# Adjacency pass of a four-layer graph network: the raw row blocks of a pair loaded by one 3 MB transfer instead of two of 1.5 MB

## The reference

```python
h = jnp.maximum(_layernorm(x, axis=-1), 0.0)
# layer 0, with e made from h by small 64 x 64 products
h = adj @ (adj.T @ e)                    # then a layer norm, gamma, beta, + residual
# layer 1
x = x + adj @ h
# layer 2: Chebyshev sum, three products by adj
T_curr = adj @ x; T_next = 2.0 * (adj @ T_curr) - T_prev    # k = 2, 3
# layer 3
a = adj + eye(n); degree = jnp.sum(a, axis=1); d_is = degree ** -0.5
out = jnp.maximum((d_is[:, None] * a * d_is[None, :]) @ (h @ W + b), 0.0)
```

## Time and profile before

| | |
|---|---|
| median of 3 runs | 1551.16 us (1549.36 to 1553.0) |
| profiled execution, its own time | 1554.13 us |
| its span, first to last instruction | 1552.3 us |
| PE busy | 1485.6 us, 96% of the span |
| DVE, ACT, POOL busy | 379.7, 256.7, 84.4 us |
| chain that ended last | PE 81%, DMA 14%, of it `raw<-in_adj_dram` 9% |
| bytes moved | 532.66 MB, 343 GB/s over the span |
| mean granted PE clock | 0.987 of full speed |

### The profile page before, as it was taken

How to read it: one execution, slowest core, us unless ns; L and a number is a source line. 1 busy time by engine, 2 the same in 40 slices (tenths; PEclk the granted TensorE clock), 3 DMA queues, 4 the chain that set the end, 5 groups by cost and what they waited for, 6 DMA issues and landing times.

```text
span 1552.3 us, 17963 instructions
## 1 busy us (share of the span) xinstructions
PE 1485.6 (96%) x7901; PEld 632.2 (41%) x7901; DVE 379.7 (24%) x383; ACT 256.7 (17%) x510; POOL 84.4 (5%) x67
## 2 busy tenths in 40 slices
PE   6998989989898989999999999999999999999996
PEld 3554545545454655323333333333333333333331
DVE  5683443434344332311101100000100021100210
ACT  2233324333333435000000000000000000000000
POOL 2300000000000004600000000000000000000000
PEclk9999999999999999999999999999999999999999
DMA  9897998979798989999999977779798845788997
GB/s 329 318 398 295 414 361 335 381 311 403 296 397 315 361 331 394 421 421 420 420 421 400 328 317 291 291 296 388 264 349 293 289 156 235 295 333 348 385 419 307
DMA packets 103218, 532.66 MB, mean 343 GB/s; under 512 B 19389, under 2 KB 19429, under 8 KB 55269
## 3 DMA queue, kind: packets, MB, share of 16 engines
q1 hardware_dynamic: 96052, 529.84, 87.1%
q10 hardware_dynamic: 7088, 1.67, 0.5%
HBM read 425.32 MB, written 106.17 MB: 342 GB/s over the span
## 4 chain that ended last, share of the span: by engine, by line
PE 81%; DMA 14%; ACT 1%; POOL 1%; DVE 1%; issue 0%; SPq 0%; ACTq 0%; POOLq 0%; DVEq 0%
PE turned L465 30%; PE acc L465 29%; PE t_acc L476 10%; PE turned L491 9%; DMA raw<-in_adj_dram 9%; DMA over_last<-adj_t 5%; ACT staged L676 1%; PE t_acc L606 1%; POOL rstd L981 1%; DMA w_in<-in_L_gnn_W_i_dram 0%; PE turned L632 0%; PE turned L638 0%; PE t_rows L616 0%; PE acc L517 0%; POOL E L998 0%
## 5 line engine op out<-in xcount | busy, mean ns | idle before, releaser
L676 ACT ACTIVATE staged<-turned 128x512 f32<-128x512 f32 x400 | 204.2, 615 | 275.0 <-PE turned L491 270.7
L809 DVE TENSOR_REDUCE deg_part<-raw 128x4 f32<-128x3072 f32 (+1 forms) x70 | 222.7, 3197 | 82.8 <-DMA raw<-in_adj_dram 82.8
L476 PE MATMUL t_acc<-raw,E 128*64 128x384 f32 (+1 forms) x1120 | 200.3, 504 | 28.1 <-DMA raw<-in_adj_dram 27.9
L491 PEld LDWEIGHTS turned<-ident,raw 128*128 128x128 f32 x1600 | 173.8, 140 | 42.6 <-issue 40.2
L491 PE MATMUL turned<-ident,raw 128*128 128x128 f32 x1600 | 190.7, 275 | 0.0
L465 PE MATMUL acc<-staged,t_cur 128*64 128x512 f32 x800 | 186.9, 601 | 2.7 <-ACT t_cur L713 1.5
L465 PE MATMUL turned<-over_last,C 128*64 128x512 f32 x680 | 153.4, 593 | 0.0
L476 PEld LDWEIGHTS t_acc<-raw,E 128*64 128x64 f32 x1120 | 82.6, 145 | 143.8 <-issue 90.5
L465 PE MATMUL turned<-over_last,R 128*64 128x512 f32 x568 | 130.4, 595 | 4.1 <-DMA over_last<-adj_t 4.1
L465 PE MATMUL acc<-over_last,R 128*64 128x512 f32 x504 | 115.3, 595 | 4.6 <-DMA over_last<-adj_t 3.3
L981 POOL TENSOR_TENSOR rstd<-rstd,minus_half 128x8 f32<-128x8 f32 (+1 forms) x30 | 43.8, 1461 | 1349.7 <-DVE rstd L800 1349.7
(11 more groups left out here) (125 smaller groups left out, 760.4 us busy)
## 6 DMA issues: line engine op xcount, KB each, us to landing
over_last<-adj_t SPq DMA_DIRECT2D x203, 1024.0 KB, 12.3
raw<-in_adj_dram SPq DMA_DIRECT2D x60, 1536.0 KB, 13.7
adj_t<-staged SPq DMA_DIRECT2D x60, 1536.0 KB, 12.7
staged<-adj_t SPq DMA_DIRECT2D x80, 1024.0 KB, 10.7
over_wide<-adj_t SPq DMA_DIRECT2D x21, 1024.0 KB, 10.3
raw<-in_adj_dram SPq DMA_DIRECT2D x10, 1024.0 KB, 10.3
adj_t<-staged SPq DMA_DIRECT2D x10, 1024.0 KB, 10.3
out_dram<-sq ACTq DMA_DIRECT2D x5, 256.0 KB, 30.4
```

The costliest lines, as they stand in the source:

```text
L476: last = nc.tensor.matmul(t_acc[h * D:(h + 1) * D, 0:columns], E[:, m * SUB + a, :], raw_of(g, m)[:, a, h * columns:(h + 1) * columns], st ...
L491: last = nc.tensor.transpose(turned[q % TURN_BANKS][:, a * P:(a + 1) * P], raw_of(g, u // 2 * 2 + b)[:, sub, c * P:(c + 1) * P], ident[:, :])
L676: nc.scalar.activation(staged_of(g, u)[:, i * B:(i + 1) * B], turned[q % TURN_BANKS][:, :], ACT.Copy) \
L809: nc.vector.tensor_reduce(deg_part[:, of(m), g], raw_of(g, m), AX.X, ALU.add).then_inc(deg_summed, 1)
```

## The change

`load_next(g, m)` now loads both blocks m and m+1 by one transfer. It is issued where the load of the even block stood, before the odd unit's store; the second load behind the store is gone. The transfer waits for the degree sum of the odd block (which comes last of the two), and both blocks' readers, PE (L476) and DVE (L809), wait for the one semaphore of the even block. The first group is loaded as before.

```diff
+        def raw_landed(g, m):
+
+            return raw_in[m if g == 0 else m // 2 * 2], 16 * (g + 1)
...
             def load_next(g, m):
 
-                sp.wait_ge(chunk_turned, chunk_no(g, m // 2 * 2 + 1, chunks(g)))
-                sp.wait_ge(deg_summed, SUM_NO[g, m])
-                src = adj_v[:, m, :, (g + 1) * GW:(g + 1) * GW + chunks(g + 1) * P]
-                sp.dma_start(raw_of(g + 1, m), src).then_inc(raw_in[m], 16)
+                sp.wait_ge(chunk_turned, chunk_no(g, m + 1, chunks(g)))
+                sp.wait_ge(deg_summed, SUM_NO[g, m + 1])
+                dst = raw_last if g + 1 == NG - 1 else raw
+                src = adj_v[:, m:m + 2, :, (g + 1) * GW:(g + 1) * GW + chunks(g + 1) * P]
+                sp.dma_start(dst[:, m:m + 2], src).then_inc(raw_in[m], 16)
...
                         load_next(g, u - 1)
                         store(g, u)
-                        load_next(g, u)
...
             def products_for_t(g, m):
 
-                pe.wait_ge(raw_in[m], g * 16 + 16)
+                pe.wait_ge(*raw_landed(g, m))
...
             def sum_rows(g, m):
 
-                dve.wait_ge(raw_in[m], g * 16 + 16)
+                dve.wait_ge(*raw_landed(g, m))
```

## The result

| | us | against before |
|---|---|---|
| before, median | 1550.74 (1549.36 to 1553.0) | |
| changed kernel, median of 4 | 1587.21 (1578.37 to 1591.07) | 1.022, 95% interval 1.0185 to 1.0255 |
| changed kernel, profiled execution | 1578.37, span 1576.5 | before 1554.13, span 1552.3 |

The change makes the kernel 36 us slower. The forecast was 1569 with a range to 1586: the direction holds, the size is twice the one named, and the median lies 1 us above the range. The kernel has also become unsteady: its executions spread over 13 us, those of before over 4.

A forecast was written before the change was run, and what follows sets the result against it. PE, busy 96% of the span, was taken as the bound. 58.9 us added less 41.4 removed, net +17.5 on the profiled 1554.13, gives 1571.6; that execution stands 3.0 above the median, so 1569, range 1549 to 1586.

The forecast's parts named there:

- Removed, 41.4 us: First stage: six boundary waits for block 9 (26.6 us), four small waits (1.3) and the slow products behind waits go.
- The idle time added, 46.9 us: PE waits before even blocks for 3 MB to land: first pairs 13.6 and 6.3, mid-group pairs 26, 512-column group 1.0 us.
- The five first pairs: PE waits before block 0 at group starts: 3.4 us in each of four groups, 6.3 us in the first.
- The twenty mid-group pairs: Four pairs in each of five groups, landing 11.9 us after issue, wanted after 10.6: 1.3 us wait each, 26 us.
- The 512-column group: Group with 1 MB blocks: first pair waits 0.5 us, middle pairs don't wait, 0.5 us added for the last.
- The slow products, 12.0 us: Products behind the five first pairs' waits run slow because the clock falls, 2.4 us each.
- Waits of this length leave the clock up: Mid-group waits of 1.3 us, with ends 0.5 and 2.2, cause no slow products.
- the clock stays up: Rival: the 3.4 us waits at group starts don't cost the clock, four times 2.4 us go; 1559 us, chance 0.17.
- 58.9: All us added: first pairs 13.6 and 6.3, slow products 12.0, mid-group pairs 26, 512-column group 1.0.
- The 3 MB are there in time: Rival: merged loads land within 10.6 us of issue, middle pairs don't wait; 1528 us, chance 0.12.
- The load finds the queue as full as now: Rival: two stores hold up the next load, mid-group waits 2.2 us, not 1.3, 18 us more; 1587 us, chance 0.15.

The follow-up runs named there:

- The order alone: Kernel before with both 1.5 MB loads of a pair issued ahead of the store, each block on its own semaphore; 1510.2 us.
- the filler: Changed kernel with 24 useless identity transposes on PE before block 0's product in five of the groups; 1575.19 us.
- the second measurement of the changed kernel: Changed kernel measured again with no edit, beside other experiments; 1586.92 us.
- the kernel with both cures: Kernel before with two 1.5 MB loads ahead of the store and PE's raw-block products one slot later; 1509.51 us.
- the two kernels with two transfers and the shared wait: Kernel before with both loads ahead of the store, PE waiting for both blocks, 1577.96 us; the same with loads also awaiting the later degree sum, 1578.61 us.

## Why the prediction was right in direction and half in size

**Removed, 41.4 us: right.** The order alone gives 40.7 us, and its row stands at 0.8 us idle and 184.7 busy, 42.9 less than before.

**The idle time added, 46.9 us: right but for one small term.** The three profiles of the changed kernel have 47.0, 49.5 and 54.0. The five first pairs, forecast at 13.6 + 6.3 = 19.9, waited 20.1, 20.1 and 21.5 us; the very first a little less than forecast (5.2 to 5.8 for 6.3), the others a little more (landings of 11.5 to 13.0 us for 11.5). The twenty mid-group pairs, forecast at 26, waited 23.8, 25.7 and 26.2, with landings after 11.9 to 12.0 us on average against 11.9. The 512-column group, forecast at 1.0, waited 2.7, 3.5 and 6.1: its middle pairs, which "don't wait" in the forecast, waited up to 1.5 us each.

**The slow products, 12.0 us: the step that failed.** The sentence was "Waits of this length leave the clock up". It took the mean wait of 1.3 us for the length of every wait. The landings in fact scatter from 10.6 to 13.9 us, so 1.3 is the mean of waits from 0 to over 3. In the three profiles the clock fell in 17 of the 20 mid-group waits of 2.17 to 3.22 us and in none that was shorter, each time at 1.4 to 1.7 us of slow products. That is 8.0, 10.2 and 9.6 us in mid-group, where the forecast had nothing. The five first pairs, where it had all of its 12.0, gave 8.2, 10.7 and 10.4. Against the 184.7 us of a run in which it never falls, the three profiles have 18.1, 22.3 and 23.0 us of slow products. In all that is 6 to 11 us above the forecast. It fell not in every such wait: 2.40 us before 204.46 left it up, 2.54 before 223.38 did not. The rival "the clock stays up" is refuted: block 0's products ran slow in 14 of 15 cases, and at full clock in four of five with the filler.

**What else is missing.** From the 1510.2 us of the order alone to the second measurement of the changed kernel, 1586.9, it is 77 us; I had 58.9. That kernel's profiled execution, at 1584.83 us, splits into 49.5 idle less the 0.8, 22.3 slow products and 3.5 outside the row. This last part seems to go with the waits: the time less the row is 1324.8 us with three tiny waits and 1328.3 with 24, some 0.15 us each, and my sum had nothing for it. It is not shown; the kernel with both cures has no wait at all and still 1326.0. The last 2 us are the distance of that execution from the median.

**The rivals.** "The 3 MB are there in time" is refuted: no 3 MB transfer of the changed kernel's three profiles landed in less than 10.5 us, and the mid-group pairs were wanted after 10.6. "The load finds the queue as full as now", 1587, has the right time but not for its reason: the mean mid-group wait was 1.2 to 1.3 us, not 2.2. In mid-group the last store landed between 1.1 us before and 3.1 us after the next load's issue, rather than 5 after it as now. The DMA view's packets row of two pairs, one that landed after 10.9 us and one after 13.1 (window from issue to landing), and of the slow one's first 2.9 us:

```profile
DMA packets 1082, 3.66 MB, mean 333 GB/s; under 512 B 16, under 2 KB 16, under 8 KB 1040
```

```profile
DMA packets 1185, 4.73 MB, mean 358 GB/s; under 512 B 32, under 2 KB 32, under 8 KB 1056
```

```profile
DMA packets 161, 0.69 MB, mean 239 GB/s; under 512 B 16, under 2 KB 16, under 8 KB 134
```

The slow one is no slower in bytes per us. By the time it lands, 1.1 MB more has been moved. The load's 3.15 MB are 1024 packets of 3 KB, which with the few under 512 B are all those under 8 KB. So the packets above 8 KB, of 12 KB each, are the stores': 42 in the fast window, 129 in the slow one. Of these, 27 lie in the first 2.9 us and are the rest of the store ahead, which had not landed yet. The other 102, 1.25 MB against 0.5, are of the stores queued behind: most of the 16 engines were done with the load and at work on the stores while the last was still at it. The Trainium skill, DMA: Bandwidth & Descriptors, section "Why a DMA increments its semaphore by 16 and not by 1", says that each engine counts for itself and that only the full count means all data landed; these rows agree.

So a part of the full queue is there after all. Over the 60 mid-group pairs of the three profiles, the load took 12.8 us on average where the store ahead landed over 2.1 us after its issue (13 pairs), and 11.4 us where that store had landed by 0.6 us (24 pairs). But landings after less than 11.1 us and after more than 13 stand in both groups, so this isn't the whole of the scatter. Why an engine lags (landings over 12.5 us) in 7 to 9 of the 20 mid-group pairs, and in the two kernels with two transfers and the shared wait in 8 and 9, was not tested.

**What a better forecast would have done.** Price a wait by its spread, not its mean. The text had 2.2 us as the upper end of a mid-group wait, close to the 2.5 us at which the trace had shown the clock fall, and still gave the twenty waits no slow products at all; the range suffered from the same omission.

## What to carry to other kernels

When transfers are merged, the first consumer waits for all the bytes: compare the landing of the whole with the time at which the first part is wanted, and if there is no slack, keep the parts on semaphores of their own and change only their order, which here brought 41 us where the merging lost 77. Where the parts must come together, move the consumer by a slot; that gave 39 us, nearly as much, and steadied the kernel. A wait on PE costs its length and, where the clock falls in it, the slow matmuls behind it, and a mean wait says little about the second: what the clock costs depends on how the waits scatter.

## What was unexpected

The granted clock fell in waits as short as 2.2 us (in the filler run, 2.04) and stayed up through others as long as 3.9. PE's timeline in the second measurement's profile of the changed kernel, and in the first's:

```profile
221.65 4.50 PE L480 MATMUL t_acc<-raw,E 128*64 128x384 f32 x16 [2.18 <-DMA raw<-in_adj_dram]
```

```profile
265.95 2.80 PE L480 MATMUL t_acc<-raw,E 128*64 128x384 f32 x16 [3.89 <-DMA raw<-in_adj_dram]
```

So the length of one wait alone doesn't decide it, and in these runs waits between 2 and 4 us went either way, which is part of why the changed kernel's time varies from execution to execution. Added PE work that computes nothing made a kernel faster by about 10 us.
